# Latent attention of a two-layer decoder: mask, negation and row maximum of a head in one VectorE instruction

## The reference

```python
kv_c = kv @ W_kvc
q_c = q @ W_dq
...
scores = (jnp.einsum('bhqd,bkhd->bhqk', q_nope, k_nope) + jnp.einsum('bhqr,bkr->bhqk', q_rope, k_rope)) * scale
k_ids = jnp.arange(lk)[None, None, :]
qs = seg_id[:, :, None]
good = (k_ids <= qs) & (k_ids >= qs - LOOKBACK)
scores = jnp.where(good[:, None, :, :], scores, NEG)
attn = jax.nn.softmax(scores, axis=-1)
out = jnp.einsum('bhqk,bkhd->bqhd', attn, v).reshape(b, lq, H * HD)
return out @ W_o
```

## Time and profile before

| | us |
|---|---|
| median of 3 runs | 752.15 |
| lowest, highest | 751.34, 752.2 |
| the profiled execution, whole | 750.47 |
| its span in the trace | 748.6 |
| TensorE busy, share of the span | 683.1 (91%) |
| VectorE | 497.8 (67%) |
| ScalarE | 317.0 (42%) |
| GpSimd | 330.2 (44%) |

### The profile page before, as it was taken

One profiled execution on the slowest core, in us unless ns is written; L12 is line 12 of the kernel. 1 busy time (PEld: TensorE's weight loads), 2 busy tenths in 40 slices (PEclk: granted clock), 3 DMA queues, 4 the chain that ended last, 5 costly groups with the idle time before them and its releaser, 6 DMA issues.

```text
span 748.6 us, 12458 instructions
## 1 busy us (share of the span) xinstructions
PE 683.1 (91%) x4626; PEld 537.3 (72%) x4626; DVE 497.8 (67%) x932; ACT 317.0 (42%) x741; POOL 330.2 (44%) x463
## 2 busy tenths in 40 slices
PE   6999889999999888687999999999979999999993
PEld 5866567876676645365788777878858888888883
DVE  5578678531144899997688888872366565656656
ACT  4665526222313745234667777770232222222220
POOL 4335418210101785633556766652244455445521
PEclk9999999999799999999999999999969999999998
DMA  7000006001003000000000000003011111111001
GB/s 265 1 2 3 2 26 256 1 1 43 1 1 80 3 17 1 2 1 0 1 1 1 2 1 1 1 2 106 1 42 40 46 43 43 53 53 43 1 1 56
DMA packets 10460, 23.28 MB, mean 31 GB/s; under 512 B 2081, under 2 KB 5218, under 8 KB 10018
## 3 DMA queue, kind: packets, MB, share of 16 engines
q1 hardware_dynamic: 10402, 22.50, 9.0%
HBM read 21.45 MB, written 1.05 MB: 30 GB/s over the span
## 4 chain that ended last, share of the span: by engine, by line
PE 75%; DVE 17%; ACT 3%; issue 2%; POOL 1%; DMA 1%; POOLq 0%; DVEq 0%; SPq 0%; ACTq 0%
PE psum L409 34%; PE psum L974 7%; DVE A L1357 7%; PE psum L983 4%; PE psum L444 4%; PE psum L996 4%; PE psum L467 3%; PE psum L769 2%; PE psum L518 2%; PE psum L560 1%; DVE A L1225 1%; PE psum L424 1%; PE psum L659 1%; DVE x_tok L1096 1%; PE psum L524 1%
## 5 line engine op out<-in xcount | busy, mean ns | idle before, releaser
L409 PE MATMUL psum<-parts 128*128 128x256 f32 (+2 forms) x1440 | 256.2, 337 | 12.2 <-DVE parts L1179 7.3
L409 PEld LDWEIGHTS psum<-parts 128*128 128x128 f32 (+1 forms) x1440 | 221.7, 194 | 41.2 <-DVE parts L1179 7.3
L1852 POOL TENSOR_SCALAR probs<-probs,row_rec 128x256 f32<-128x256 f32 x128 | 60.3, 484 | 59.5 <-DVE row_rec L1169 56.8
L1536 ACT ACTIVATE probs<-probs,neg_max 128x256 f32<-128x256 f32 x128 | 63.6, 500 | 47.7 <-DVE neg_max L1162 47.7
L1802 ACT ACTIVATE A<-psum 128x512 f32<-128x512 f32 x44 | 26.3, 598 | 129.7 <-PE psum L409 129.7
L1357 DVE TENSOR_TENSOR_SCAN A<-decay,psum 128x256 f32<-128x256 f32 x128 | 75.4, 661 | 3.5 <-PE psum L814 3.5
L1482 DVE TENSOR_TENSOR A<-A,psum 128x512 f32<-128x512 f32 x44 | 30.3, 688 | 70.3 <-PE psum L409 70.3
L1991 POOL CAST parts<-C 128x512 fp32r<-128x512 f32 (+1 forms) x44 | 31.1, 706 | 100.5 <-PE psum L409 90.2
L974 PE MATMUL psum<-C,A 128*128 128x256 f32 x256 | 70.2, 398 | 0.0
L1158 DVE TENSOR_TENSOR probs<-psum,ctxT 128x512 f32<-128x512 f32 x64 | 44.1, 689 | 21.1 <-PE psum L974 19.5
L1992 POOL TENSOR_TENSOR parts<-C,parts 128x512 fp32r<-128x512 f32 (+1 forms) x44 | 54.9, 1248 | 3.5
(11 more groups left out here) (218 smaller groups left out, 1223.2 us busy)
## 6 DMA issues: line engine op xcount, KB each, us to landing
C<-in_experts SPq DMA_DIRECT2D x22, 384.0 KB, 3.0
A<-in_w_o SPq DMA_DIRECT2D x1, 2048.0 KB, 12.4
x_tok<-in_x_tok SPq DMA_DIRECT2D x1, 1024.0 KB, 7.2
ctxT<-in_ctxT SPq DMA_DIRECT2D x1, 1024.0 KB, 10.4
out<-x_tok SPq DMA_DIRECT2D x8, 128.0 KB, 1.8
A<-in_w_uqT SPq DMA_DIRECT2D x1, 768.0 KB, 6.1
xT<-in_xT SPq DMA_DIRECT2D x2, 256.0 KB, 4.0
C<-in_wqk SPq DMA_DIRECT2D x1, 512.0 KB, 4.3
```

What stands on the lines that cost most here:

```text
L409: ins = mm(o, left[l], right[r], start=first and n == 0, stop=last and n == 2, skip_group_check=True)
L1536: last = af(slot, scores, ACT.Exp, bias=neg_max[:, u % RING[n], j:j + 1], accum_out=row_sum[:, u % RING[n], j:j + 1])
L1852: last = pool.tensor_scalar(pr, pr, row_rec[:, u % RING[n], j:j + 1], 1.0, ALU.mult, ALU.mult)
```

## The change

Each unit's mask addition and negated maximum become two VectorE instructions, one for each head. `tensor_tensor_reduce` computes out = (scores + mask) x -1.0 and, beside it, the minimum of out, started from 3.0e38; so `probs` holds negated masked scores and `neg_max` the negated maximum, as before. The exponential reads the negated scores with scale -1.0. TensorE's wait before it writes over a bank of scores is now for `max`, the end of the unit's second instruction; the semaphore `masked` is gone, and with it VectorE's wait for its own mask addition.

```diff
--- before.py
+++ after.py
@@ -452,7 +452,7 @@
                 for u in range(U + LAG[n] + 2 + 2 * AT_ONCE[n]):
                     if u < U:
                         if u >= len(ring):
-                            pe.wait_ge(sem(n + ("exp" if causal_keys else "masked")), u - len(ring) + 1)
+                            pe.wait_ge(sem(n + "max"), u - len(ring) + 1)
                         scores(u, bank[ring[u % len(ring)]]).then_inc(sem(n + "sc"), 1)
                     if filler:
                         filler(u)
@@ -1146,21 +1146,17 @@
                     if 0 <= v < U and v % 2 == 1:
                         copy_probs(dve, n, v, causal_keys, lambda o, i: cp(o, i), "d")
                     if u < U:
-                        keys = (u % 2 + 1) * P if causal_keys else 256
                         s3 = bank[ring[u % len(ring)]][:, :].rearrange("p (j k) -> p j k", j=2)
                         dve.wait_ge(sem(n + "sc"), u + 1)
                         if u % 16 == 0:
                             dve.wait_ge(sem("mask"), 2 * (u // 16) + 2)
-                        if not causal_keys:
-
-                            if u >= RING[n]:
-                                dve.wait_ge(sem(n + "tr"), u - RING[n] + 1)
-                            tt(probs_slot(n, u), s3, bc(mask_m[:, 2 * (u // 16) + u % 2, :], 2), ALU.add
-                               ).then_inc(sem(n + "masked"), 1)
-                            s3 = probs_slot(n, u)
-                            dve.wait_ge(sem(n + "masked"), u + 1)
-                        dve.tensor_reduce(neg_max[:, u % RING[n], :], s3[:, :, 0:keys], axis=AX, op=ALU.max,
-                                          negate=True).then_inc(sem(n + "max"), 1)
+                        if u >= RING[n]:
+                            dve.wait_ge(sem(n + "tr"), u - RING[n] + 1)
+                        for j in range(2):
+                            last = dve.tensor_tensor_reduce(
+                                probs_slot(n, u)[:, j, :], s3[:, j, :], mask_m[:, 2 * (u // 16) + u % 2, :], -1.0, 3.0e38,
+                                ALU.add, ALU.min, neg_max[:, u % RING[n], j:j + 1])
+                        last.then_inc(sem(n + "max"), 1)
                     v = u - SUMS[n]
                     if 0 <= v < U:
                         dve.wait_ge(sem(n + "exp"), v + 1)
@@ -1533,7 +1529,7 @@
                         for j in range(2):
                             slot = probs_slot(n, u)[:, j, 0:keys]
                             scores = bank[ring[u % len(ring)]][:, j * 256:j * 256 + keys] if causal_keys else slot
-                            last = af(slot, scores, ACT.Exp,
+                            last = af(slot, scores, ACT.Exp, scale=-1.0,
                                       bias=neg_max[:, u % RING[n], j:j + 1],
                                       accum_out=row_sum[:, u % RING[n], j:j + 1])
                         last.then_inc(sem(n + "exp"), 1)
```

## The result

The changed kernel takes 746.19 us (median of 7 runs, 745.13 to 749.57); the kernel of before, run beside it, 751.04 (747.83 to 752.2). The ratio is 0.995, with a 95% interval of 0.993 to 0.997: faster, by 3.8 us (2.3 to 5.3); the two medians alone differ by 4.85 us. Two later comparisons of the same file gave 0.9969 (0.9951 to 0.9986) and 0.9929 (0.9905 to 0.9953). The forecast was 749.3 us, in a range from 747.3 to 752.7.

The account below looks back on a forecast made before the run. TensorE was taken to bound steady state, VectorE's gain counting only in seven of 64 units: 1.26 + 0.78 + 0.42 + 0.42 = 2.88 us, so 752.15 - 2.88 = 749.27, say 749.3 us, range 747.3 to 752.7.

Parts of the forecast that it names:

- the price of a unit: VectorE's time from scores to maxima in one unit: 1.00 us after the change against 1.42, a gain of 0.42.
- the level: Time of the kernel of before from which the gain was subtracted: 752.15 us, the median of the runs.
- The seven units: Units 2, 3, 4, 7, 8, 10 and 62 have VectorE time on the path; the other 57 give nothing.
- place (c): Stage's end, unit 62 at 497.25 us: gain 0.42 of TensorE's 0.72 us idle.
- the low end (0.87): One unit's VectorE time with passes and accumulator reads all overlapped: 0.87 us, a gain of 0.55.
- the series case: Accumulator reads wait for passes to drain: 1.14 us per unit, gain 0.28, 1.96 us in all, 750.2 us; chance 0.18.
- place (a): Units 2, 3 and 4, from 341.69 us, VectorE's chain ahead of POOL's rows: 3 x 0.42 = 1.26 us gained.
- B: Piece from TensorE's first L424 to its second; units 7 and 8 forecast to gain 0.78 us, TensorE's idle time.
- C: Piece from the second L424 to L872; unit 10 forecast to gain 0.42 of TensorE's 0.52 us idle.
- D: Piece from L872 to the first output product L996; unit 62 forecast to gain 0.42 us.
- The smaller edits: TensorE's wait now for the maxima, and exponentials reading negated scores with scale -1.0: both forecast to cost nothing.
- Rival 4: Granted clock after TensorE's idle time at 352 to 356 us changes: 1.68 us more won (747.6) or lost (750.9); chance 0.08.

Follow-up runs that it names:

- e_all_but_seven: Changed kernel with the old two instructions kept in units 2, 3, 4, 7, 8, 10 and 62, new ones in the other 57; 752.18 us, ratio 1.0013.
- e_pad2: Changed kernel plus two VectorE row maxima that nobody reads in each of units 12 to 60; 746.82 us, ratio 0.9946.
- e_only_seven: Changed kernel with the new instruction only in units 2, 3, 4, 7, 8, 10 and 62, the old two elsewhere; 747.07 us, ratio 0.9959.
- e_series: Changed kernel with VectorE waiting on its first head's accumulator before the second head's pass; 0.89 us per unit, stage 167.8 us from unit 0's mask.

## Why the prediction was right or wrong, point by point

The account of what bounds the kernel and of the path was right in the main. What failed are two terms of the sum: the price of a unit (1.00 us, measured 0.78) and the level (752.15 us, later 751.04 and 750.50).

*What bounds the kernel: right.* VectorE's time in steady state is worth nothing: e_all_but_seven has 57 faster units and no gain, e_pad2 has 32 us more work and no loss.

*The seven units: right but for two.* Units 3, 4, 7, 8, 10 as stated. The sum counted unit 2 in full, saying that the scores were there in time; what it left out is the residual behind unit 2, which needs products that TensorE makes after those scores. It gives some 0.1 us. And unit 63 was left out; by the rows of e_only_seven it is what adds to unit 62, which alone gives 0.36, to make the 0.63 of place (c).

*The price of a unit: the step of the working that failed.* The prediction took 1.00 us, g = 0.42; measured were 0.78 and 0.64. The pass was priced right (0.414 from L1393; 0.421 measured). The read was priced by L1169 at 0.155 us, and even the low end (0.87) gave it 0.07 us of VectorE's queue and its full length at the end. It takes 0.083 us (the median of the group) and no place in the queue. Halfway to the series case was too far: made in series on purpose, the unit takes 0.89 us. ScalarE's row, 0.49 us from head to head against 0.50 for the instruction, did say that the read is free; it was quoted and then given half its weight.

*The sum.* With 0.64: place (a) 1.37 (forecast 1.26), B 0.91 (0.78), C 0.62 (0.42), D 0.63 (0.42), together 3.53 instead of 2.88. B and C exceed TensorE's printed idle times (0.78 and 0.52), which the prediction took as ceilings, by 0.1 us each. The ends of matmuls are modelled in the profile, so a bracket can be too short; that this is the cause was not tested.

*The smaller edits: right.* TensorE's wait for the maxima and the exponentials' scale cost nothing: e_all_but_seven has the wait in all units and the scale in 57, and its A, B, C and D are those of before within 0.02 us; and the mean of an exponential is 500 ns before and after.

*The rule weighed against the rows.* The rule of the Trainium skill (page "VectorE: DVE Perf Modes", section "Rules for kernel authors"), to keep the number of operations low rather than to fuse, did not decide here: the instructions doubled from two to four per unit and the time fell by 45%, since two of the four are free and the other two take 0.42 us each where the old two took 0.69. The count of an accumulator output as two instructions (the Trainium skill, the same page, section "Two Vector instructions with no wait between them") is what the trace shows, as two rows; by time it was one.

*Rival 4, the clock: open.* It was given 8%, with "Nothing in the rows says which". In the two traces of the first comparison the clock fell both times, so their difference owes it nothing. Over all traces the fall came in 2 of 7 with 2.7 us of idle time against 7 of 8 with 3.3, too few to call the link shown.

*The level: the larger part of the miss.* The forecast was set against 752.15, the median of three runs, though the text noted that the profiled execution was 1.68 us lower. Beside the changed kernel the kernel of before took 751.04, and later 750.50. So of the 3.1 us between forecast and result, 1.1 to 1.7 are the level, 0.65 the gain (3.53 instead of 2.88), and the rest is within the scatter of medians: the changed kernel gave 746.19, 747.95 and 746.16. The right price of a unit alone, 752.15 - 3.53 = 748.6, would not have reached the result. The low end, 747.3, was 752.15 less 3.50 and a part of a clock fall. Against 750.50 the same sum would have given 747.6, and a range as wide, 745.7 to 751.1, would have held the result.

## What to carry to other kernels

Ask of a faster instruction at which few units it ends a wait, and test that by making it fast only there and only elsewhere: two runs settled 3.2 of 3.5 us here. Where the granted clock scatters from run to run, compare traces piece by piece between named instructions; such pieces agreed to 0.03 us where medians moved by 2 us. Take the level from more than three runs where a forecast is to hold to a microsecond: here it was off by 1.1 to 1.7 us, for a gain of 3.5. And look at what the engines do while another idles: moving one POOL step up took piece A from 12.10 to 10.32 us, and the ratio from 0.9969 (0.9951 to 0.9986) and 0.9929 (0.9905 to 0.9953) to 0.9903 (0.9872 to 0.9934).

## What the runs showed of the hardware that was not expected

- An accumulator read on VectorE takes 77 to 85 ns and started together with the instruction behind it in 126 of 128 cases; that instruction started 0.35 us after a pass of 0.42 us.
- The pass that adds, negates and keeps a running minimum over 256 elements takes 391 to 426 ns, like a plain addition from PSUM (0.414 us), and not like the scan (0.661 us).
- A wait of VectorE on its own accumulator between the heads cost 0.12 us in e_series.
- With VectorE always busy an instruction cost less than its printed length: four of 0.41 us held it for 1.31 us. 64.2 us of such padding lengthened the stage by 12.2 us; the rest fell into time in which VectorE had been idle.
- TensorE's clock fell behind an idle time of 3.3 us in 7 of 8 traces, of 2.8 us in the one there is and of 2.7 us in 2 of 7, and a fall cost 1.5 to 2.6 us.
